# A state-space stage: the mixing matrix as one vector product over four heads, and x times dt as a GpSimd product of its own

## The reference, cut to what matters

```python
dt = jax.nn.softplus(dt + dt_bias)
x_scaled = x * dt[..., None]
A_dt = A[None, None, :] * dt
Y_diag = jnp.einsum('bclhn,bcshn,bhcls,bcshp->bclhp', C, B, Lmat, X)   # X is x_scaled, Lmat = exp(segsum(A_dt))
states = jnp.einsum('bclhn,bhcl,bclhp->bchpn', B, decay_states, X)
Y_off  = jnp.einsum('bclhn,bchpn,bhcl->bclhp', C, states, state_decay_out)
y = Y_diag + Y_off + x * D
g = y * jax.nn.silu(z)
y = g * lax.rsqrt(jnp.mean(g * g, axis=-1, keepdims=True) + EPS) * norm_w      # then the output projection
```

## Time and profile before

| what | value |
|---|---|
| median of 3 runs | 1367.37 us (1366.83 to 1368.35) |
| the profiled execution | 1377.32 us, its span 1375.6 us |
| TensorE busy | 1281.5 us, 93% of the span |
| VectorE busy | 912.1 us, 66% |
| ScalarE busy | 608.8 us, 44% |
| GpSimd busy | 464.7 us, 34% |
| chain that ended last | PE 61%, DVE 22%, issue 9%, ACT 6%, POOL 1% |

### The profile page before, as it was taken

One profiled execution on the slowest core, in us unless ns is written; L12 is line 12 of the kernel. 1 busy time (PEld: TensorE's weight loads), 2 busy tenths in 40 slices (PEclk: granted clock), 3 DMA queues, 4 the chain that ended last, 5 costly groups with the idle time before them and its releaser, 6 DMA issues.

```text
span 1375.6 us, 20883 instructions
## 1 busy us (share of the span) xinstructions
PE 1281.5 (93%) x7224; PEld 1068.2 (78%) x7224; DVE 912.1 (66%) x1734; ACT 608.8 (44%) x1125; POOL 464.7 (34%) x568
## 2 busy tenths in 40 slices
PE   6699999999999999999899999999999799999994
PEld 6577888888888888888667767767767687888884
DVE  3486645453534444446588678678676799999997
ACT  3243323232323232334666666666664444444441
POOL 1244300000000000000354554453444566677775
PEclk9899999999999999999899999999999999999997
DMA  4122101000000001000000110010110101010000
GB/s 179 51 77 96 31 1 31 1 16 16 1 31 0 30 0 46 0 16 1 28 26 18 35 43 9 33 43 8 35 43 16 39 1 31 30 30 30 30 16 31
DMA packets 30404, 41.38 MB, mean 30 GB/s; under 512 B 2433, under 2 KB 22913, under 8 KB 30209
## 3 DMA queue, kind: packets, MB, share of 16 engines
q1 hardware_dynamic: 30336, 40.53, 9.0%
HBM read 27.94 MB, written 12.58 MB: 29 GB/s over the span
## 4 chain that ended last, share of the span: by engine, by line
PE 61%; DVE 22%; issue 9%; ACT 6%; POOL 1%; DVEq 1%; DMA 1%; ACTq 0%; POOLq 0%; SPq 0%; PEldq 0%
PE bank L44 18%; PE bank L46 17%; PE bank L45 17%; DVE acc L1153 3%; DVE dab L1313 2%; DVE beats L1297 2%; PE bank L1666 2%; PE bank L1672 2%; DVE dh L1279 2%; DVE rows_out L1346 1%; DVE mag L984 1%; DVE rank L1302 1%; PE bank L1655 1%; DVE st L1036 1%; PE bank L1634 1%
## 5 line engine op out<-in xcount | busy, mean ns | idle before, releaser
L1060 DVE TENSOR_TENSOR hb<-gl,bank 128x512 f32<-128x512 f32 x128 | 87.9, 687 | 200.1 <-PE bank L46 197.5
L670 ACT ACTIVATE hh<-hb 128x512 fp32r<-128x512 f32 x128 | 80.9, 632 | 182.2 <-DVE hb L1060 182.2
L709 ACT ACTIVATE gl<-bank 128x512 f32<-128x512 f32 x128 | 76.4, 597 | 181.8 <-PE bank L46 181.7
L1023 DVE TENSOR_TENSOR hl<-hb,hh 128x512 fp32r<-128x512 f32 x128 | 95.6, 747 | 84.5 <-ACT hh L670 84.5
L520 POOL TENSOR_TENSOR veb<-mvb,eps 128x4 f32<-128x4 f32 x8 | 1.8, 228 | 378.7 <-DVE mvb L1040 378.7
L44 PE MATMUL bank<-xt_l,w_h 128*128 128x512 f32 x256 | 103.8, 406 | 17.9 <-DVE xt_l L1023 15.6
L653 POOL TENSOR_TENSOR dhl<-dab,dhh 128x512 fp32r<-128x512 f32 x64 | 100.3, 1590 | 31.1 <-ACT dhh L670 31.1
L44 PE MATMUL bank<-at_l,w_hi_a 128*128 128x512 f32 x256 | 102.9, 402 | 1.3 <-DVE at_l L1023 1.0
L46 PE MATMUL bank<-xt_h,w_h 128*128 128x512 f32 x256 | 101.9, 398 | 0.0
L46 PE MATMUL bank<-at_h,w_hi_a 128*128 128x512 f32 x256 | 101.8, 398 | 0.0
L45 PE MATMUL bank<-xt_h,w_l 128*128 128x512 f32 x256 | 101.8, 398 | 0.0
(11 more groups left out here) (222 smaller groups left out, 3781.2 us busy)
## 6 DMA issues: line engine op xcount, KB each, us to landing
xg<-x_scratch SPq DMA_DIRECT2D x16, 512.0 KB, 3.9
xall<-in_x SPq DMA_DIRECT2D x8, 512.0 KB, 7.3
xg<-in_xt SPq DMA_DIRECT2D x8, 512.0 KB, 4.8
x_scratch<-rows_out SPq DMA_DIRECT2D x8, 512.0 KB, 3.2
x_scratch<-rows_out SPq DMA_DIRECT2D x16, 256.0 KB, 2.2
out<-rows_out SPq DMA_DIRECT2D x8, 512.0 KB, 3.2
wq<-in_codes SPq DMA_DIRECT2D x12, 256.0 KB, 2.6
sc<-in_scales SPq DMA_DIRECT2D x12, 256.0 KB, 2.9
```

The source lines that it names most:

```text
L670: return act.activation(dst, src, ACT.Copy)
L709: act.activation(gl[:, n % 2], ps_gate[n % 2][:], ACT.Gelu_apprx_tanh).then_inc(s_gelu, 1)
L1023: return dve.tensor_tensor(dst, src, hi.bitcast(F32), ALU.subtract)
L1060: dve.tensor_tensor(hb[:, n % 2], gl[:, n % 2], ps_up[n % 2][:], ALU.mult).then_inc(s_h, 1)
```

## The change

For each chunk, the four DVE instructions that multiplied a head's decay table by dt and by the masked CB become one instruction over all four heads. It multiplies the 128 x 512 decay table by the masked CB, which is read four times from PSUM. The factor dt moves to x: POOL gets a new instruction per chunk, `xsd` = `xtk` times dt, in a new buffer, and TensorE's diagonal product reads `xsd` in place of `xtk` and waits for its semaphore too. On POOL the new instruction stands first in the chunk's code, ahead of `masked_decay`, `halo_terms` and `inv_rms`, and with it go the waits for `xtk` of this chunk and for the `yo` sum of the chunk before.

```diff
@@ POOL, step
                 for c in range(NT):
                     k, u = NT * s + c, c % 2
                     before = not isinstance(k, int) or k > 0
+                    pool.wait_ge(c_xtk, k + 1 + 1)
+                    pool.wait_ge(c_yo2, k + 1)
+                    if not isinstance(k, int) or k > 1:
+                        pool.wait_ge(c_y, k - 1)
+                    pool.tensor_tensor(xsd[:, u], xtk[:, u], dtv[:, b, c].unsqueeze(2).broadcast_to([P, HEADS, HEADDIM]),
+                                       ALU.mult).then_inc(c_xsd, 1)
                     if nxt and c == 2:
                         masked_decay(nxt[0], 0)
                         masked_decay(nxt[0], 1)
                     if nxt and c == 0:
                         halo_terms(nxt[0], nxt[1])
                     if before:
                         inv_rms(k - 1, 1 - u)
-                    pool.wait_ge(c_xtk, k + 1 + 1)
-                    pool.wait_ge(c_yo2, k + 1)
                     pool.tensor_tensor(xd[:, u], xtk[:, u], d4[:].unsqueeze(2).broadcast_to([P, HEADS, P]),
                                        ALU.mult).then_inc(c_xd, 1)
@@ DVE, step
                     dve.wait_ge(c_gm, k + 1 + 1)
                     dve.wait_ge(c_e, k + 1)
-                    for h in range(HEADS):
-                        m = dve.scalar_tensor_tensor(mm_[:, u, h], ee[:, c, h], dtv[:, b, c, h:h + 1], small[:, P:2 * P],
-                                                     ALU.mult, ALU.mult)
-                    m.then_inc(c_m, 1)
+                    dve.tensor_tensor(mm_[:, u], ee[:, c], small[:, P:2 * P].unsqueeze(1).broadcast_to([P, HEADS, P]),
+                                      ALU.mult).then_inc(c_m, 1)
@@ PE, step
                     pe.wait_ge(c_m, k + 1)
+                    pe.wait_ge(c_xsd, k + 1)
                     pe.wait_ge(c_g1, k + 1)
                     for h in range(HEADS):
-                        mm = pe.matmul(ps_y[:, h * HEADDIM:(h + 1) * HEADDIM], mm_[:, u, h], xtk[:, u, h],
+                        mm = pe.matmul(ps_y[:, h * HEADDIM:(h + 1) * HEADDIM], mm_[:, u, h], xsd[:, u, h],
                                        start=True, stop=True)
```

More of the change, by code:

```diff
@@ L204, in build @@
         dw = cs("dw", [P, 2, NT, HEADS])
+        xsd = cs("xsd", [P, 2, HEADS, HEADDIM])
         xd = cs("xd", [P, 2, HEADS, HEADDIM])
@@ L305, in build @@
         c_dw = sem("state_weight_ready")
+        c_xsd = sem("x_dt_ready")
         c_m = sem("mixing_ready")
```

## The result

The changed kernel takes 1376.36 us (median of 18 runs, 1372.62 to 1379.9); the kernel before, in the same series, 1373.24 us (18 runs, 1366.83 to 1375.65). The ratio is 1.0034, with a 95% interval of 1.002 to 1.0048: slower by about 4.6 us, with the interval from 2.7 to 6.6. (The two medians alone lie 3.1 us apart.) I had forecast 1368.4 us, a rise of 1.0 us over the 1367.37 of three runs. Those three are counted among the 18 and lie at their low end. So the forecast missed by 8 us: some 6 of them are in the base, and the rest is in the size of the effect.

The account below looks back on a forecast made before the run. The chain was taken to leave TensorE for DVE in chunk 1 of groups 0 to 6. Six groups at +0.15 us (-0.42 + 0.57) and group 3 at some +0.1 gave +1.0 on 1367.37: 1368.4 us, range 1364.3 to 1373.0.

Parts of the forecast that it names:

- the base: The starting time, 1367.37 us, to which the summed effect of +1.0 us was added.
- The mixing matrix: DVE's four mm_ instructions, 1.02 us, become one of 0.60: 0.42 saved a chunk, 2.94 us on the chain.
- The product: x times dt on POOL: 1.04 us a chunk, 33 us more busy time; TensorE's added wait priced at nothing.
- The order in chunk 1: POOL runs xsd, then au; block 2's short DVE instruction is delayed 0.57 us and goes ahead of the second au.
- The six groups: The groups on the chain other than group 3: each -0.42 + 0.57 = +0.15 us, together +0.90.
- the forecast order: Group 3: block 1 delayed 0.42 us by the yo sum, block 2 by 0.09 behind xsd; net some +0.1 us.
- The idle stretch ahead of the z projection: TensorE's wait in groups 0 to 6, forecast to grow from 1.57 to some 2.1 us.
- Chunk 1 as the only one that counts: mm_ is on the chain only in chunk 1 of groups 0 to 6; the other 25 savings end in DVE's idle time.
- the clock: Rival: longer TensorE idle draws the low clock in groups 0 and 3, 3.2 us more, 1371.6 us; chance 0.2.
- The sum: Chain effects over groups 0 to 6: +0.90 for six groups and +0.1 for group 3, +1.0 us.
- the hold: POOL's au product delays DVE's short instruction of convolution block 2 by 0.57 us in six groups, 0.09 in group 3.
- The rival's total: The clock rival's outcome: 3.2 us more from low clock in groups 0 and 3, giving 1371.6 us; chance 0.2.

Follow-up runs that it names:

- the second profiled execution of after: Profile taken when the changed kernel was run again with no edit, beside other experiments: 1376.63 us, 1.003 to before.
- tables first: Changed kernel with one move: on POOL in chunk 2 the two au products stand ahead of x times dt again: 1359.94 us, 0.9907 to before.
- chunk 1 only: Fused mm_ and xsd in chunk 1 of every group only, au products ahead of xsd, other chunks as before: 1357.08 us, 0.9899 to before.
- before with the pair: Kernel before plus a never-read TensorE matmul pair ahead of the z projection in chunk 2, groups 0 to 6: 1363.11 us, 0.9938.
- after with the pair: Changed kernel plus a never-read TensorE matmul pair ahead of the z projection in chunk 2, groups 0 to 6: 1363.93 us, 0.9942 to before.
- two doses: Kernel with the change in chunk 1 only, plus two never-read DVE instructions ahead of mm_ in chunk 1, groups 0 to 6: 1368.53 us, 0.9976 to before.
- chunks 0, 2 and 3 only: Fused mm_ and xsd in these chunks, chunk 1 as before, au products ahead of xsd: 1372.47 us, 1.0017 to before.
- product alone: Kernel before with xsd on POOL as in the change and TensorE waiting for it; four mm_ instructions and xtk kept: 1379.88 us, 1.0048.
- the two kernels with a hold and no saving: Before with xsd and its wait added, four mm_ kept (1.0048), and before with only a POOL wait for xtk ahead of the au products (1.0057).

## Why the prediction was wrong, step by step

**Right.** The mixing matrix: 0.59 us for 1.02. The product: 1.04 us, and TensorE's wait for it sets nothing. The order in chunk 1: xsd, then au, with the halo instruction let in between the two au products, and held 0.5 us. The six groups, with one correction: in groups 0, 1, 2, 5 and 6 block 2's instruction takes 0.72 to 0.80 us, but in group 4 it was not held (0.20), and in group 3 only a little (0.27). In these two groups the same instruction was held in blocks 3 and 4 instead, up to 1.20 us, by POOL's yo sum (line 618, 851.99 to 853.26 in group 3) and by xsd of chunk 3, of which I had nothing. In group 3 the forecast order came true, 0.62 us in block 1 and 0.27 in block 2, but that is in part luck: the second profiled execution of after has no hold in block 1 there, 0.72 us in block 2 as in the other groups, and none over 0.80 us. The idle stretch ahead of the z projection: 2.10 us forecast, 2.10 measured. Chunk 1 as the only one that counts.

**Two steps failed: the base, and the clock.** The larger part of the miss is the step "1367.37 + 1.0": before's median is 1373.24 us, 5.9 more than the base I took (more below). The step that failed in the effect is the clock. The prediction put it among the rivals: "If both get it, 2 x 1.6 = 3.2 more", at 0.2. The sum took a microsecond on the chain for a microsecond of the end. The runs show that in chunk 1 it is worth four or more: the saving of 2.9 us returns 13 to 14.5 us where nothing is held (0.9907, 0.9894, 0.9899), and the hold, 2.8 us of direct delay in after's groups, takes 1.0034 - 0.9907 = 1.3%, 17 us, from the kernel with the tables first. The result of +4.6 us is the rest of two terms three to four times its size. My sum of +1.0 had the same two terms at -2.9 and +3.9.

The rival's total, +1.0 and +3.2, comes close to +4.6, but not by its account. It let the two groups that had no low stretch behind the wait get one. Group 0 did, in both profiles of after. Group 3 did in the second profile only, and there group 5 lost both of its own.

**Why the rest is small, and positive.** TensorE's idle time around the wait has two pieces in before: 0.46 us ahead of the output transposes of line 1600, and 1.57 us ahead of the z projection, 2.03 together. The prediction looked at the second alone. The table has both in group 2, and the low stretches beside the time of the same, profiled, execution. Before's profiled execution is slower than all of its 18 timed runs, so its 13 is more than usual:

| kernel | first piece | second piece | low stretches in groups 0 to 6 | profiled execution, us | ratio |
|---|---|---|---|---|---|
| chunk 1 only | none | 1.57 | 2 | 1357.66 | 0.9899 |
| tables first | 0.29 | 1.57 | 3 | 1359.79 | 0.9907 |
| before with the pair | 0.50 | 0.71 | 4 | 1363.77 | 0.9938 |
| after with the pair | 0.28 | 1.24 | 4 | 1363.16 | 0.9942 |
| two doses | 0.46 | 1.56 | 8 | 1368.11 | 0.9976 |
| chunks 0, 2 and 3 only | 0.36 | 1.57 | 11 | 1370.79 | 1.0017 |
| before | 0.46 | 1.57 | 13 | 1377.32 | 1 |
| after | none | 2.10 | 14 | 1379.11 | 1.0034 |
| product alone | 0.51 | 2.10 | 13 | 1379.86 | 1.0048 |

The time follows the number of low stretches closely. It follows the idle pieces less well: before with the pair has the least idle time and is not the fastest; it lacks the saving on DVE. The fusion takes away the first piece, and the hold adds as much to the second. With 2.03 and 2.10 us the two kernels stand close together, near the end where nearly every group has its two low stretches. From there the two kernels with a hold and no saving lose about twice its size (6.6 to 7.8 us for 3.3 to 4.0). A gain brings four to five times its size. My reading is that few groups are left to lose. That the +4.6 is a direct term of at most 1 us with the clock on top is argued, and no run of its own shows it. The mean granted clock of after is lower by 0.001 to 0.003. Among before's own runs 0.001 goes with 0.7 to 0.9 us, so I estimate 1 to 3 us from the clock, 2 to 4 with the direct term, and the interval of the ratio is 2.7 to 6.6.

**The base.** I carried the difference to the median of three runs. The 18 runs of before range over 9 us, and their time follows the mean clock of the execution: 1364.8 us at 0.973 and 1376.5 at 0.960 to 0.963 in the runs beside the experiments. The kernels with few low stretches hardly scatter: the one with the change in chunk 1 only ran from 1354.99 to 1357.66. I had seen a profiled execution 10 us above the three runs, with no cause for it, and should have widened the range upward by it.

**What stays open.** Which group gets a low stretch changes from one execution to the next, and no run here tells what decides it. Two doses restore before's idle pieces in group 2 to 0.01 us, and yet its profile has 8 low stretches for 13, and its interval ends just under 1. Some of the stretches that go away lie in parts of the group that no edit touched, and how much of the gain is from each place was not separated.

**The best version.** The fused matrix with the tables ahead of the product beats both kernels: 0.9907 in all chunks, 0.9899 in chunk 1 only, 0.9893 with the matmul pair added. The three can't be told apart. The plainest, three lines of after moved, is the one to take.

## What to carry to other kernels

When a product is given a place in a queue, list what stood behind that place: here two products that could run at once came to stand behind a wait, and landed on another engine's short instruction. Before summing microseconds on a chain that leaves TensorE, look at the granted clock behind its idle stretches: where it falls in some groups and not in others, the kernel is at the edge, and time ahead of that wait can be worth several times itself (here four to five times for a gain, about twice for a loss). A base that scatters by more than the effect is such a sign too, and three runs are no base for it.

## What the runs showed of the hardware

- Useless work on TensorE can pay: 7 matmul pairs of 1.0 us, put into a wait of 1.57 us, gave 0.62% (0.9918 to 0.9958), and the low stretches went from 13 to 4.
- DVE's 3-column add of two SBUF operands takes 0.15 to 0.19 us in before, and up to 1.20 us in after, where it starts inside a POOL product. In group 2 it ends 0.03 us after the first au product of 1.02 us, and does not wait for the second one behind it.
- A piece of 3.4 us at TensorE's lower clock costs about 1.6 us: the same group work took 48.34, 49.93 and 51.47 us with none, one and two of them.
- A broadcast of one PSUM operand over four heads costs DVE nothing to speak of: 0.59 us from start to start for 512 columns, as for gt_l with no broadcast. Four scalar_tensor_tensor instructions of 128 columns, which multiply by dt as well, take 1.02 us.
